# A mixture-of-experts layer on one core: result rows of full width, loads and stores of two chunks, and scatters without pauses

## What is computed

```python
h = layernorm(x)
q = h @ Wq.T + bq;  k = l2norm(ctx @ Wk.T + bk);  v = l2norm(ctx @ Wv.T + bv)   # 16 heads of 8
x = x + q @ (k.T @ v)                      # one 8x8 state for each sequence and head
w = softmax(layernorm(x) @ W_router.T + b_router)
# every expert takes the first 1280 tokens that chose it, in token order, and drops the rest
for e in range(8):
    t = first_1280_tokens_with_e_in_top2(w, e)
    x_out[t] += relu(layernorm(x)[t] @ W_in[e]) @ W_out[e] * w[t, e]
return x + x_out
```

## Time and profile before

| what | value |
|---|---|
| median of 3 runs | 404.75 us (403.3 to 411.94) |
| the profiled execution, its own time | 407.75 us |
| its span, first to last instruction | 406.0 us |
| busy: PE, DVE, ACT, POOL | 304.8, 228.3, 213.6, 224.7 us |
| scatters of the first part | 96, 1.0 us each on POOL |
| adds of the second part | 80, 1.56 us each on POOL |
| mean granted TensorE clock | 0.846 of full speed |

### The profile page before, as it was taken

How to read it: one execution, slowest core, us unless ns; L and a number is a source line. 1 busy time by engine, 2 the same in 40 slices (tenths; PEclk the granted TensorE clock), 3 DMA queues, 4 the chain that set the end, 5 groups by cost and what they waited for, 6 DMA issues and landing times. The chain is left out here.

```text
span 406.0 us, 6826 instructions
## 1 busy us (share of the span) xinstructions
PE 304.8 (75%) x2247; PEld 255.1 (63%) x2247; DVE 228.3 (56%) x892; ACT 213.6 (53%) x431; POOL 224.7 (55%) x197
## 2 busy tenths in 40 slices
PE   4987778685868759673675999797979896989700
PEld 3555556363645537452543999797979796989600
DVE  4588766978676586774647555253535352545200
ACT  1778645765474364673313567364747463666500
POOL 3000455055764675666720086877868686768682
PEclk8699998897975977988556899898989996999955
DMA  6124513344341442411103234646374646354332
GB/s 201 38 80 120 167 57 112 85 124 121 123 123 43 123 129 63 126 36 52 36 26 96 106 30 36 153 38 151 35 154 37 152 36 156 33 100 36 31 32 19
DMA packets 33299, 34.68 MB, mean 85 GB/s; under 512 B 4701, under 2 KB 24794, under 8 KB 33264
## 3 DMA queue, kind: packets, MB, share of 16 engines
q0 software_dynamic: 14592, 11.16, 18.9%
q1 hardware_dynamic: 18096, 22.75, 18.4%
q10 hardware_dynamic: 576, 0.33, 0.3%
HBM read 18.82 MB, written 16.58 MB: 87 GB/s over the span
## 5 line engine op out<-in xcount | busy, mean ns | idle before, releaser
L381 POOL DMA_INDIRECT slots_dram<-rows,place_no x96 | 96.4, 1004 | 113.1 <-DVE place_no L729 49.8
L421 POOL DMA_INDIRECT out_dram<-y_sb,token x80 | 124.8, 1560 | 60.3 <-ACT y_sb L524 31.8
L814 DVE SCALAR_TENSOR_TENSOR hid_lo<-ps,hid_hi 128x1024 fp32r<-128x1024 f32 x40 | 49.0, 1225 | 63.5 <-ACT hid_hi L514 60.7
L514 ACT ACTIVATE hid_hi<-ps 128x1024 fp32r<-128x1024 f32 x40 | 41.1, 1029 | 43.6 <-PE ps L962 38.2
L878 PE MATMUL ps<-wkv_sb,ct_sb 128*128 128x256 f32 x128 | 46.7, 467 | 13.7 <-issue 5.5
L960 PE MATMUL ps<-xgt_hi,wi_hi 128*128 128x256 f32 x160 | 50.7, 317 | 0.3 <-DVE xgt_lo L797 0.3
L981 PE MATMUL ps<-hid_hi,wo_hi 128*128 128x256 f32 x160 | 49.8, 311 | 0.2 <-DVE hid_lo L814 0.2
L878 PEld LDWEIGHTS ps<-wkv_sb,ct_sb 128*128 128x128 f32 x128 | 25.4, 241 | 36.9 <-issue 33.3
L962 PE MATMUL ps<-xgt_hi,wi_lo 128*128 128x256 f32 x160 | 47.5, 297 | 0.0
L961 PE MATMUL ps<-xgt_lo,wi_hi 128*128 128x256 f32 x160 | 47.4, 296 | 0.0
L982 PE MATMUL ps<-hid_lo,wo_hi 128*128 128x256 f32 x160 | 46.0, 288 | 0.0
(11 more groups left out here) (120 smaller groups left out, 626.1 us busy)
## 6 DMA issues: line engine op xcount, KB each, us to landing
xg<-slots_dram SPq DMA_DIRECT2D x8, 576.0 KB, 4.1
ct_sb<-ctx_t_dram SPq DMA_DIRECT2D x16, 256.0 KB
out_dram<-rows SPq DMA_DIRECT2D x16, 256.0 KB
x_sb<-x_dram SPq DMA_DIRECT2D x15, 256.0 KB
wi_sb<-w_in_dram SPq DMA_DIRECT2D x8, 256.0 KB
wo_sb<-w_out_dram SPq DMA_DIRECT2D x8, 256.0 KB
slots_dram<-rows,place_no POOLq DMA_INDIRECT x96
out_dram<-y_sb,token POOLq DMA_INDIRECT x80
```

What stands on the lines that cost most here:

```text
L381: pool.indirect_dma_start(slots[:, :], bass.IndirectOffsetOnAxis(ap=place_no[:, u % PLACES_RING, j:j + 1], axis=0), rows[:, c % ROWS_RING, ...
L421: pool.indirect_dma_start(out[:, :], bass.IndirectOffsetOnAxis(ap=token[:, e, j:j + 1], axis=0), y_sb[:, e % 2, j, :], None, compute_op=AL ...
L514: act.activation(hid_hi[:, i % 2, :], [ps0, ps1][i % 2][:, :], ACT.Relu).then_inc(hid_high, 1)
L814: dve.scalar_tensor_tensor(hid_lo[:, i % 2, :], [ps0, ps1][i % 2][:, :], 0.0, hid_hi[:, i % 2, :].bitcast(F32), ALU.max, ALU.subtract).the ...
```

## The change

- **Result rows.** `out_dram` has 144 columns in place of 128. A store sends whole rows (576 bytes each) with gates and token number, of which the host cuts the first 128 columns. Rows of `out_dram` and x are in another order on the host, so that eight rows of a pair of chunks lie behind one another for each partition: 4608 bytes.
- **Loads and stores.** x, context and stores go by units, two chunks in one DMA. The x and context rings have 6 buffers. A store now waits for `place_ready` of its unit (it needs gates and token numbers), and stands behind the next unit's load in SP's queue. The last store stands behind the load of expert 0's slots.
- **Semaphores** of loads and stores are one for each unit.
- **Adds.** The token numbers are multiplied by 9, and the index of an add counts pieces of 16 values, since a row has 9 of them; each add still sends 128 rows of 128 values.
- **No pace.** `keep_pace` is gone: POOL issues the 8 or 16 scatters of a unit one behind the other.

```diff
--- before.py
+++ after.py
@@ -26,9 +26,10 @@
 
 
 ROW_GATE, ROW_TOKEN, ROW = D, D + EXPERTS, D + EXPERTS + 8
+PARTS = ROW // 16
 NO_SLOT = 16384
 LN_EPS, L2_EPS = 1e-5, 1e-12
-RING = 4
+RING = 6
 ROWS_RING = 8
 PLACES_RING = 4
 IT = INNER // P
@@ -210,10 +211,11 @@
         bias_loaded = sem("bias_loaded")
         consts_made = sem("consts_made")
         ones_made = sem("ones_made")
-        x_loaded = [sem(f"x_loaded{b}") for b in range(RING)]
-        ct_loaded = [sem(f"ct_loaded{b}") for b in range(RING)]
+
+        x_loaded = [sem(f"x_loaded{u}") for u in range(LAST + 1)]
+        ct_loaded = [sem(f"ct_loaded{u}") for u in range(LAST + 1)]
         rows_sent = [sem(f"rows_sent{u}") for u in range(LAST + 1)]
-        x1_stored = [sem(f"x1_stored{b}") for b in range(ROWS_RING)]
+        x1_stored = [sem(f"x1_stored{u}") for u in range(LAST + 1)]
         dummies_stored = sem("dummies_stored")
 
         x_normed, x_turned, xnt_made = map(sem, ("x_normed", "x_turned", "xnt_made"))
@@ -247,8 +249,10 @@
         yt_made, y_turned, down_done, y_made = map(sem, ("yt_made", "y_turned", "down_done", "y_made"))
 
 
-        x_c = x.rearrange("(c p g) d -> c p g d", g=G, p=P)
-        out_c = out[0:TOKENS, :].rearrange("(c g p) d -> c p g d", g=G, p=P)
+        x_q = x.rearrange("(q p k g) d -> q p k g d", p=P, k=2, g=G)
+        out_q = out[0:TOKENS, :].rearrange("(q p k g) r -> q p k g r", p=P, k=2, g=G)
+
+        out_parts = out.rearrange("n (q w) -> (n q) w", q=PARTS)
         slots_e = slots.rearrange("(e p j) r -> e p j r", e=EXPERTS, p=P)
 
         def norms_of(s):
@@ -259,20 +263,27 @@
 
         @block.sync
         def _(sp):
-            def load(c):
-                if not valid(c):
+            def load(u):
+                first, number = UNITS[u]
+                last, b = first + number - 1, first % RING
+                if last >= RING:
+                    after(sp, x1_made, last - RING)
+                    after(sp, kv_projected, last - RING)
+                if u > 0:
+                    sp.dma_start(x_sb[:, b:b + number], x_q[first // 2][:, first % 2:first % 2 + number]) \
+                        .then_inc(x_loaded[u], 16)
+                sp.dma_start(ct_sb[:, b:b + number, :], ctx_t[:, first * TOK:(first + number) * TOK]
+                             .rearrange("d (k t) -> d k t", k=number)).then_inc(ct_loaded[u], 16)
+
+            def store(u):
+
+                if u is None:
                     return
-                if c >= RING:
-                    after(sp, x1_made, c - RING)
-                    after(sp, kv_projected, c - RING)
-                sp.dma_start(ct_sb[:, c % RING, :], ctx_t[:, c * TOK:(c + 1) * TOK]).then_inc(ct_loaded[c % RING], 16)
-                sp.dma_start(x_sb[:, c % RING], x_c[c]).then_inc(x_loaded[c % RING], 16)
-
-            def store(c):
-                if not valid(c):
-                    return
-                after(sp, x1_made, c)
-                sp.dma_start(out_c[c], rows[:, c % ROWS_RING, :, 0:D]).then_inc(x1_stored[c % ROWS_RING], 16)
+                first, number = UNITS[u]
+                b = first % ROWS_RING
+                after(sp, place_ready, u)
+                sp.dma_start(out_q[first // 2][:, first % 2:first % 2 + number], rows[:, b:b + number]) \
+                    .then_inc(x1_stored[u], 16)
 
             def load_weights(e):
                 par = e % 2
@@ -289,19 +300,22 @@
             sp.dma_start(bkv_sb[:, :], bkv.rearrange("(a d) -> a d", a=1).broadcast_to([P, 2 * D])) \
                 .then_inc(bias_loaded, 16)
             sp.dma_start(wkv_sb[:, :], wkv_t).then_inc(kv_consts_loaded, 16)
-            sp.dma_start(ct_sb[:, 0, :], ctx_t[:, 0:TOK]).then_inc(ct_loaded[0], 16)
+            load(0)
             sp.dma_start(br_sb[:, :], br.rearrange("(a d) -> a d", a=1).broadcast_to([P, EXPERTS])) \
                 .then_inc(small_loaded, 16)
             for s in STEPS:
-                load(s + 2)
-                store(s - 1)
+                for u in range(1, LAST + 1):
+                    if s == max(-1, UNITS[u][0] - 3):
+                        load(u)
+                store(second_half(s - 1))
                 if s == 2:
                     sp.wait_ge(pads_cleared, 1)
-                    sp.dma_start(out[TOKENS:TOKENS + P, :], zeros[:, :]).then_inc(dummies_stored, 16)
+                    sp.dma_start(out[TOKENS:TOKENS + P, 0:D], zeros[:, :]).then_inc(dummies_stored, 16)
                     for e in range(2):
                         load_weights(e)
             sp.wait_ge(slots_ready, 1)
             load_slots(0)
+            store(LAST)
             sp.wait_ge(xg_loaded[0], 16)
             load_slots(1)
             for e in range(2, EXPERTS):
@@ -340,44 +354,19 @@
                       allow_small_or_imprecise_dtypes=True)
             pool.iota(slot_no[:, :], pattern=[[1, SLOT_TILES]], base=0, channel_multiplier=SLOT_TILES,
                       allow_small_or_imprecise_dtypes=True)
-            pool.iota(token_no[:, :], pattern=[[P, TILES]], base=0, channel_multiplier=1)
-
-            pool.iota(token[:, :, :], pattern=[[0, EXPERTS], [0, SLOT_TILES]], base=TOKENS, channel_multiplier=1)
+            pool.iota(token_no[:, :], pattern=[[DUO * P * PARTS, TILES // DUO], [PARTS, DUO]], base=0,
+                      channel_multiplier=DUO * PARTS)
+
+            pool.iota(token[:, :, :], pattern=[[0, EXPERTS], [0, SLOT_TILES]], base=TOKENS * PARTS,
+                      channel_multiplier=PARTS)
             pool.memset(zeros[:, :], 0.0)
             pool.memset(rows[:, :, :, ROW_TOKEN + 1:ROW], 0.0)
             pool.drain().then_inc(pads_cleared, 1)
-
-            def keep_pace(u, pair):
-
-
-                c = sum(UNITS[u]) + 1
-                if pair == 1 and valid(c):
-                    after(pool, x1_made, c)
-                if pair == 2 and valid(c + 2):
-                    after(pool, q_projected, c + 2)
-                if pair == 3 and valid(c + 3):
-                    after(pool, kv_projected, c + 3)
-                if pair == 4 and valid(c + 1):
-                    after(pool, attended, c + 1)
-                if pair == 5 and valid(c + 2):
-                    after(pool, state_summed, c + 2)
-                if pair == 6:
-                    if valid(c + 3):
-                        after(pool, q_projected, c + 3)
-                    elif valid(c + 1):
-                        after(pool, x1_made, c + 1)
-                if pair == 7:
-                    if valid(c + 4):
-                        after(pool, kv_projected, c + 4)
-                    elif valid(c + 2):
-                        after(pool, x1_made, c + 2)
 
             def scatter(u):
                 first, number = UNITS[u]
                 for j in range(scatters(u)):
                     c = first + j // (G * TOP_K)
-                    if j % 2 == 0:
-                        keep_pace(u, j // 2)
                     pool.indirect_dma_start(
                         slots[:, :], bass.IndirectOffsetOnAxis(ap=place_no[:, u % PLACES_RING, j:j + 1], axis=0),
                         rows[:, c % ROWS_RING, j // TOP_K % G, :], None, bounds_check=SLOTS - 1, oob_is_err=False,
@@ -407,8 +396,8 @@
                     with pool.Else():
                         pool.sem_inc(slots_ready, 1)
 
-            for b in range(ROWS_RING):
-                pool.wait_ge(x1_stored[b], 16 * (CHUNKS // ROWS_RING))
+            for u in range(LAST + 1):
+                pool.wait_ge(x1_stored[u], 16)
             pool.wait_ge(dummies_stored, 16)
             for e in range(EXPERTS):
                 after(pool, gates_made, e)
@@ -419,7 +408,7 @@
                     if j % PAIR == 0:
                         after(pool, y_made, e * GROUPS + j // PAIR)
                     pool.indirect_dma_start(
-                        out[:, :], bass.IndirectOffsetOnAxis(ap=token[:, e, j:j + 1], axis=0),
+                        out_parts, bass.IndirectOffsetOnAxis(ap=token[:, e, j:j + 1], axis=0),
                         y_sb[:, e % 2, j, :], None, compute_op=ALU.add,
                     ).then_inc(rows_added[e % 2], 16)
             pool.drain()
...
@@ -992,7 +981,7 @@
 
     nc = bacc.Bacc("TRN2", target_bir_lowering=False, num_devices=1)
     arrays = {
-        "x": np.asarray(x).reshape(CHUNKS, G, P, D).transpose(0, 2, 1, 3).reshape(TOKENS, D),
+        "x": np.asarray(x).reshape(TILES // DUO, DUO, P, D).transpose(0, 2, 1, 3).reshape(TOKENS, D),
         "ctx_t": np.asarray(ctx_1024).reshape(TOKENS, D).T,
         "wq_t": np.asarray(L0_xattn_Wq).T,
         "bq": np.asarray(L0_xattn_bq),
@@ -1006,8 +995,9 @@
     arrays = {name: np.ascontiguousarray(a) for name, a in arrays.items()}
     drams = [nc.dram_tensor(name + "_dram", a.shape, F32, kind="ExternalInput").ap() for name, a in arrays.items()]
 
-    out = nc.dram_tensor("out_dram", (TOKENS + P, D), F32, kind="ExternalOutput").ap()
```

(8 more changed lines are left out.)

4 lines of the change are left out of this document (2 added, 2 removed).

## The result

| | before | changed |
|---|---|---|
| median (range) | 404.78 us (403.3 to 411.94, 4 runs) | 459.81 us (455.69 to 463.31, 4 runs) |
| ratio | | 1.132 (95% interval 1.123 to 1.141) |
| profiled run, its span | 407.75, 406.0 us | 463.31, 461.5 us |
| mean granted clock in the span | 0.846 | 0.809 |

The change loses 55 us where 11 were forecast. The direction was right, the size wrong, and the time lies outside the range.

The account below looks back on a forecast made before the run. The prediction took a chain of signals between engines, lengthened with scatters, to bound the first part, and POOL's adds the second. Its terms summed as 404.75 + 3.8 + 7.6 + 0 = 416 us, with 386 to 432 us for 8 times in 10.

Parts of the forecast that it names:

- The hold: First part: engines wait on "remote" while scatters run one behind another; something with scatters adds 2.3 to 7.3 us per two steps.
- the signs for "right": Runs of 16 scatters at 1.27 us, copy and mask idle 5 us and more, five stretches 26 us and up, clock below 0.8.
- PE's signal is raised late: First part: the prediction's account of a hold, with DVE's mask and ACT's copy waiting 4.5 us and more during scatters.
- No pace, +11.4 us: Scatters without pauses in the first part: 3.8 us for the first stretch and 7.6 us for the other four.
- The high end, 5 x 7.6 us: Upper bound for removing the pace: one more hold of the longest kind in each of five stretches, 38 us.
- The cover of the scatters: First part: the ring of 8 chunks, five steps long, keeps POOL's own scatter time off the path.
- Loads of two chunks, wide stores: 0: SP's loads and stores: fewer, larger transfers change nothing on the path, since no step waits for them.
- Adds: 0: Second part's 80 adds: same rows and as many descriptors, taken as 0; upper bound 7.6 us if rows land later.
- rival 3: Second part: adds cost 7.6 us more through slower landing at the 576 byte pitch, 412 us; chance 0.07.
- Hand-over: 0: From the last scatters to the first add: slots asked for perhaps 2 us sooner, gaining at most a few tenths; taken as 0.
- Rival 1: First part: narrow stores and many SP DMAs with scatters cause the holds, wide ones remove them; 390 us, chance 0.33.
- Rival 2: Whole kernel: nothing measurable changes, the pace costs what it gives and wide stores are hidden; 404 us, chance 0.18.

Follow-up runs that it names:

- e11: The kernel before (narrow loads, stores and adds) with only the paces taken out, on a chip with holds: 460.0 us, ratio 1.135.
- e12: The changed kernel (wide loads, stores and adds) with the paces put back, on a chip with holds: 407.8 us, ratio 1.012.
- e13: The changed kernel with different pauses by unit (none, memsets, waits for landings), on a chip with holds: 420.6 us, one run.
- e16: The changed kernel with POOL memsets of another size in each unit from 2 to 6, on a chip with holds: 412.2 us, one run.
- e7: The changed kernel itself against the kernel before, on a chip without holds: 375.2 us, ratio 0.996.
- e1: The kernel before with only the paces taken out, on a chip without holds: 375.5 us, ratio 1.000.
- e8: The kernel before with only the paces taken out, on a chip without holds: 373.8 us, ratio 0.994.
- e4: The changed kernel with a 128x768 memset on POOL behind each scatter, on a chip without holds: 419.9 us, ratio 1.119.
- e18: The kernel before, its paces replaced by a 128x768 memset behind every second scatter, on a chip without holds: 395.5 us, ratio 1.046.
- e5: The changed kernel again beside the kernel before, on a chip with holds: 459.1 us, ratio 1.128.
- e6: The kernel before, unchanged, run for its own profile on a chip with holds: 411.1 us, one run.
- e17: The changed kernel with a 128x768 memset on POOL behind every second scatter, on a chip with holds: 396.5 us, ratio 0.985.
- e10: The changed kernel with POOL waiting for its own landings ahead of a unit's fifth, ninth and thirteenth scatter, chip without holds: 407.3 us, ratio 1.079.
- e14: The changed kernel with POOL memsets of another size in each unit from 2 to 6, on a chip without holds: 390.8 us, one run.
- e15: The changed kernel with a 128x768 memset on POOL behind every second scatter, on a chip without holds: 395.1 us, ratio 1.048.

## Why the prediction was right or wrong

- *The hold is what decides, and it comes with unbroken scatters*: right in kind; e11 (narrow, no pace, 460.0 us) and e12 (wide, paced, 407.8 us) show it. Of the signs for "right", the runs of 16 at 1.27 us came in, distances over 26 us in all five stretches, and a clock of 0.64 to 0.76 in them. The waits on "remote" came in for the copy of x1t in four of the five stretches (14.1 to 15.8 us) and for the mask in three (10.6 to 14.2 us). Too narrow was "PE's signal is raised late": signals of DVE are late as well (e13, and 3.84 us at ACT's line 442 in the kernel before).
- *No pace, +11.4 us*: **this step failed**. The term measured +54.0 us in the same five stretches. The high end, 5 x 7.6 us, was too low as well. Two readings were wrong. The longest hold of the earlier trace rows was taken as the length of a hold; but it was the length of what was left of a run of eight until the next pause, and it ended 1.5 us behind that run (189.99, then 191.46 and 191.52). Without pauses the run lasts 20.3 us, and so the hold can last that much longer: 10 to 16 us of waiting in the changed kernel. And the mean was scaled by POOL's busy share, 56% against 66% and 76%, as if the loss grew evenly with it. It doesn't: e16 shows nothing at mean distances of 1.59 and 1.68 us, waits of 2.8 us at 1.49 and of up to 13.4 us at 1.43, and the changed kernel long holds in every run at 1.27. In hindsight, a working from the earlier trace rows would have come nearer: suppose that each of the five runs holds from a few us after its start until its end, so some 13 us a stretch instead of the 3 to 7 that the paced stretches lie above 20.4 us; (20.4 + 13 to 15) x 5 is 167 to 177 us against 128.2, a loss of 39 to 49 us, an estimate from those rows and the run's 20.3 us. It is still 5 to 15 us short of the 54, and what makes up the rest wasn't looked for.
- *The cover of the scatters*: "nobody waits for the scatters of units 0 to 5" was right, and so was that a faster POOL gains nothing by itself. e7, the whole change on a chip without holds, is at 0.996.
- *Loads of two chunks, wide stores: 0*. Right. No wait for x or context stands among the steps of the changed kernel, SP's queue carries half the packets (8928), and e11 is as slow without them.
- *Adds: 0*. Right: 1.54 and 0.30 us, and 18.5 us in seven waits between experts against 18.3. Two of the seven are over the 3 us named as the sign of rival 3 (3.09 and 3.20), but the kernel before has one of 3.13. Rival 3 is out, and with it the 7.6 us that the rule of the Trainium skill on pieces off a 256 byte border would have given (DMA: Bandwidth & Descriptors, How a descriptor splits into AXI transactions): rows at a pitch of 576 bytes landed as fast as rows at 512.
- *Hand-over: 0*. Right in effect: 289.83 - 276.93 = 12.9 us from the last places to the first add, and 12.9 us before.
- *Rival 1 (narrow stores make the holds)*: out. e11, with all narrow stores, and the changed kernel, with none, hold alike. The sign in its favour, the adds that hold nothing, has another reason that fits: adds come 1.84 us apart, scatters without a pause 1.27 us.
- *Rival 2 (nothing changes)*: true on a chip without holds (e7; e1 and e8 for the missing pace alone), a case that the prediction had no place for. There the rule of the Trainium skill that neither PE nor ACT waits for a DMA at SBUF (SBUF — State Buffer, SBUF: two separate sides) agrees with the trace (e7 has no wait on "remote"). On the other chips most of the waiting stands between the end of one engine's instruction and the start of the next one's, where the rule says nothing; no run here shows at which point of that way it arises.

What stays open: what the two kinds of chip differ in, and what the engines and the scatters share. It can be the path of the signals, or the supply of instructions to the engines, as the slow instructions of PE (e16) and DVE (e13) would have it; no experiment here separates the two. It isn't shown either that the chip itself decides, and not the time of the run: one chip was met twice (e1 to e4, and e18 43 minutes later) and held nothing both times, but no other chip is known to have been met twice, and groups with and without holds came by turns. How closeness and number of scatters in a row act together is a reading of single runs, not a proof.

## What to carry to other kernels

A wait that seems needless on an engine which issues transfers in a row may be there to space them out. Before taking it away, read what arrives right behind each of its pauses: if waits on "remote" end there, their length without the pause goes by the length of the run that is left, not by the longest one seen. If the spacing is all that is wanted, make it with work of the engine's own (here 0.75 us after two scatters), and time it on more than one chip: here this pause took 14% off the changed kernel's time where signals were held (the two met different chips of that kind) and cost 5% where they weren't.

## What was not expected of the hardware

- Eight groups of runs met two kinds of chip. On four (the pair above, e5 and e6, e11 to e13, e16 and e17) the kernel before took 405 to 408 us and with scatters 1.27 us apart engines waited up to 15.8 us on "remote" (the copy of x1t, changed kernel); on the others (e1 to e4, e7 to e10, e14 and e15, e18) it took 376 to 377 us, and none of the kernels profiled there has a wait on "remote". The duration of a scatter was 0.97 us on both.
- On a chip with holds the granted clock falls with them: 0.64 to 0.76 in the changed kernel's stretches, 0.86 to 0.92 in those of e7. PE was busy 49 to 60% of the first and 77 to 78% of the second. Its mean over the span was 0.809 against 0.901.
- With scatters 1.43 us apart PE's instructions themselves came late: two of them 0.73 us apart, and sixteen state products in 5.9 us in place of 1.16 us (e16). With scatters 1.27 us apart DVE's came 1.4 us apart (e13).
